# Twenty bf16 identity matmuls on TensorE at the start of each attention call

## The chip, the core and the metric

The kernel runs on one core of one Trainium2 chip. The metric is the device time of one execution in microseconds (us). Three runs of the kernel before took 1405.46, 1410.10 and 1411.19 us; their median is 1410.1 us. All computation is in one launch.

## The reference, cut to what matters

The reference is a decoder of four layers on x of 8 x 128 x 128 (batch B = 8, sequence S = 128, width D = 128). Each layer has an attention-like block, a cross block with a context of the same size, and a feed-forward block:

```python
x = x + L0_attn(layernorm(x), ...)        # mamba scan
x = x + L0_xattn(layernorm(x), ctx, ...)  # attention, rotary, masks     -> call 0
x = x + L0_ffn(layernorm(x), ...)         # experts
x = x + L1_attn(layernorm(x), ...)        # causal, relative positions   -> call 1
x = x + L1_xattn(...); x = x + L1_ffn(...)
x = x + L2_attn(layernorm(x), ...)        # causal, rotary               -> call 2
x = x + L2_xattn(...)
x = x + L2_ffn(layernorm(x), ...)         # holds a causal attention     -> call 3
x = x + L3_attn(layernorm(x), ...)        # two causal attentions        -> calls 4 and 5
x = x + L3_xattn(...); x = x + L3_ffn(...)
```

The change touches the softmax attentions, with 16 heads of 8 elements each:

```python
att = einsum("bhtd,bhsd->bhts", q, k) / sqrt(8) + bias   # 8 x 16 matrices of 128 x 128
out = einsum("bhts,bhsd->bhtd", softmax(masked(att)), v)
```

## The kernel before

The program is a row of stages, each a block in which the five engines run their own instruction queues and meet through semaphores; at a block's end all engines meet. The six attentions all go through one function, `attend` (L508), once per call. In front of it `attention_inputs` (L413) projects queries, keys and values; behind it `out_project` (L667) projects the result.

`attend` works through 32 units: a unit is one batch element and one group of four heads (HG = 4), that is four score matrices of 128 x 128, one bank of 128 x 512 f32 in PSUM. Four banks hold scores, two hold turned probabilities (`PT`), one holds the weighted sums (`PO`) and one, `back`, holds these sums turned back to token rows. All eight banks are in use. A unit passes through these steps:

- `add_bias` (TensorE, L546): mask or position bias, as bf16 matmuls of 512 columns into `scores`; one per unit with 64 rows in call 0, three per unit in call 1, one per unit (`identb` by a mask) in calls 2 to 5;
- `score` (TensorE, L553): queries against keys, f32, 32 rows of the array, into the same bank. The keys `KH` come from GpSimd (L537), spread by a head mask;
- `highest` (VectorE, L614): reduction for the softmax's shift; `exp` (ScalarE, L648): four activations;
- `turn` (TensorE, L561): four f32 transposes into `PT`; `copy` (VectorE, L620): to SBUF;
- `weigh` (TensorE, L570): 4 matmuls with the values into `PO`.

Once per batch element ScalarE evacuates `PO` (L656), TensorE turns it back into `back` (`turn_back`, L579), and VectorE divides by the sums of exponentials (L625, L626), reading `back`.

The order on TensorE is written out by hand. Biases and scores of units 0 to 3 come first. Then each pass of a loop takes two units: turn u and u+1, biases of u+4 and u+5, in some passes `turn_back`, scores of u+4 and u+5, and weighing of u-2 and u-1. So the passes u = 0 and u = 2 are the ones without a weighing or with the first one. TensorE's instructions start strictly in this order; a wait at the head holds all that is behind it. `back` is first written in the pass u = 6 (`turn_back(0)`, as `u % NG == 2 and u >= NG`).

`m.identb` (L163, filled at L283) is the 128 x 128 identity in bf16; `bcast_mid(x, n)` (L234) repeats x n times along the free dimension.

Of the kernel before, what the change touches and what calls it, by code (L numbers as in the profile page):

```python
# [27 lines left out]
HG = 4  # L28
# [205 lines left out]
def bcast_mid(ap, n):  # L234

    return ap.unsqueeze(1).to_broadcast([ap.shape[0], n, ap.shape[1]])


def bcast_last(ap, n):

    return ap.unsqueeze(2).to_broadcast([ap.shape[0], ap.shape[1], n])


def start_stage(nc, m):
# [263 lines left out]
def attend(nc, m, QT, KT, O, bias, beside=None):  # L508

    call = m.n_attn
    m.n_attn += 1
    U0, B0 = call * B * NG, call * B
    UNITS = B * NG
    with ExitStack() as ctx:
        sb = lambda name, shape, dt=F32: ctx.enter_context(nc.sbuf_tensor(f"{name}_a{call}", shape, dt))
        ps = lambda name, shape: ctx.enter_context(nc.psum_tensor(f"{name}{call}", shape, F32))
        KH = [sb(f"KH{i}", [D, HG, S]) for i in range(2)]
        shifted = [sb(f"shifted{i}", [S, HG, S]) for i in range(4)]  # L520
        PTs = [sb(f"PTs{i}", [S, HG, S]) for i in range(4)]
        POs = [sb(f"POs{i}", [128, NG, S]) for i in range(2)]
        nmax, rsum = sb("nmax", [S, 4, HG]), sb("rsum", [S, 2, H])
        scores = [ps(f"scores{i}_", [S, HG, S]) for i in range(4)]
        PT = [ps(f"PT{i}_", [S, HG, S]) for i in range(2)]
        PO, back = ps("PO", [128, NG, S]), ps("back", [S, NG, 128])
        block = ctx.enter_context(nc.Block())
        ident = m.w("ident")

        @block.gpsimd  # L530
        def _(pool):
            for b in range(B):
                if beside is not None and b >= 2:
                    beside(pool, b - 2)
                if b >= 2:
                    pool.wait_ge(m.scored, U0 + (b - 1) * NG)
                nc.gpsimd.tensor_tensor(KH[b % 2][:], bcast_mid(KT[:, b * S:(b + 1) * S], HG),  # L537
                                        bcast_last(m.w("head_mask"), S), ALU.mult).then_inc(m.kh_ready, 1)

        @block.tensor  # L540
        def _(pe):
            def add_bias(u):
                if u >= 4:
                    pe.wait_ge(m.exped, U0 + u - 3)
                for k, (w, x) in enumerate(bias(u % NG, u // NG)):
                    nc.tensor.matmul(scores[u % 4][:], w, x, start=(k == 0), stop=False)  # L546

            def score(u):
                g, b = u % NG, u // NG
                rows = slice(32 * g, 32 * g + 32)  # L550
                if g == 0:
                    pe.wait_ge(m.kh_ready, B0 + b + 1)
                nc.tensor.matmul(scores[u % 4][:], QT[rows, b * S:(b + 1) * S], KH[b % 2][rows, :, :], start=False,  # L553
                                 stop=True).then_inc(m.scored, 1)

            def turn(u):
                pe.wait_ge(m.exped, U0 + u + 1)
                if u >= 2:
                    pe.wait_ge(m.pt_copied, U0 + u - 1)
                for j in range(HG):  # L560
                    t = nc.tensor.transpose(PT[u % 2][:, j, :], shifted[u % 4][:, j, :], ident)  # L561
                t.then_inc(m.p_turned, 1)

            def weigh(u):
                g, b = u % NG, u // NG
                pe.wait_ge(m.pt_copied, U0 + u + 1)
                if g == 0 and b >= 1:
                    pe.wait_ge(m.po_copied, B0 + b)
                for j in range(HG):
                    t = nc.tensor.matmul(PO[32 * j:32 * j + 32, g, :], m.V[:, b, g * HG + j, :], PTs[u % 4][:, j, :],  # L570
                                         start=True, stop=True)
                t.then_inc(m.weighed, 1)

            def turn_back(b):
                pe.wait_ge(m.po_copied, B0 + b + 1)
                if b >= 1:
                    pe.wait_ge(m.out_done, B0 + b)
                for g in range(NG):
                    t = nc.tensor.transpose(back[:, g, :], POs[b % 2][:, g, :], ident)  # L579
                t.then_inc(m.turned_back, 1)  # L580

            for u in (0, 1):
                add_bias(u)
            for u in (0, 1):
                score(u)
            for u in (2, 3):
                add_bias(u)
            for u in (2, 3):
                score(u)
            for u in range(0, UNITS, 2):  # L590
                turn(u)
                turn(u + 1)
                if u + 4 < UNITS:
                    add_bias(u + 4)
                    add_bias(u + 5)
                if u % NG == 2 and u >= NG:
                    turn_back(u // NG - 1)
                if u + 4 < UNITS:
                    score(u + 4)
                    score(u + 5)  # L600
                if u >= 2:
                    weigh(u - 2)
                    weigh(u - 1)
            weigh(UNITS - 2)
            weigh(UNITS - 1)
            turn_back(B - 1)

        @block.vector
        def _(dve):
            def highest(u):  # L610
                if u >= 4:
                    dve.wait_ge(m.exped, U0 + u - 3)
                dve.wait_ge(m.scored, U0 + u + 1)
                nc.vector.tensor_reduce(nmax[:, u % 4, :], scores[u % 4][:], AX.X, ALU.min).then_inc(m.maxed, 1)  # L614

            def copy(u):
                dve.wait_ge(m.p_turned, U0 + u + 1)
                if u >= 4:
                    dve.wait_ge(m.weighed, U0 + u - 3)
                nc.vector.tensor_copy(PTs[u % 4][:], PT[u % 2][:]).then_inc(m.pt_copied, 1)  # L620

            def normalise(b):
                dve.wait_ge(m.turned_back, B0 + b + 1)
                po = back[:].rearrange("p g (j e) -> p (g j) e", j=HG)
                m.dve_steps.done(dve, nc.vector.reciprocal(rsum[:, b % 2, :], po[:, :, DH]))  # L625
                nc.vector.tensor_tensor(O[:, b, :].rearrange("p (h d) -> p h d", h=H), po[:, :, 0:DH],  # L626
                                        bcast_last(rsum[:, b % 2, :], DH), ALU.mult).then_inc(m.out_done, 1)

            for u in range(4):
                highest(u)  # L630
            for u in range(0, UNITS, 2):
                copy(u)
                copy(u + 1)
                for k in (u + 4, u + 5):
                    if k < UNITS:
                        highest(k)
                if u % NG == 2 and u > NG:
                    normalise(u // NG - 1)
            normalise(B - 1)

        @block.scalar
        def _(act):
            def exp(u):
                if u >= 4:
                    act.wait_ge(m.p_turned, U0 + u - 3)
                act.wait_ge(m.maxed, U0 + u + 1)
                for j in range(HG):
                    t = nc.scalar.activation(shifted[u % 4][:, j, :], scores[u % 4][:, j, :], ACT.Exp, scale=-1.0,  # L648
                                             bias=nmax[:, u % 4, j:j + 1])
                t.then_inc(m.exped, 1)  # L650

            def evacuate(b):
                act.wait_ge(m.weighed, U0 + (b + 1) * NG)
                if b >= 2:
                    act.wait_ge(m.turned_back, B0 + b - 1)
                nc.scalar.activation(POs[b % 2][:], PO[:], ACT.Copy).then_inc(m.po_copied, 1)  # L656

            m.load_table(act, ACT.Exp)
            for u in range(0, UNITS, 2):
                exp(u)  # L660
                exp(u + 1)
                if u % NG == 2 and u >= NG:
                    evacuate(u // NG - 1)
            evacuate(B - 1)
# [1666 lines left out]
```

## Time and profile before

| | |
|---|---|
| median of three runs | 1410.1 us |
| the profiled execution's own time | 1418.91 us |
| its span, first to last instruction | 1417.0 us |
| TensorE matmul, weight load | 1106.5 us (78%), 802.9 us (57%) |
| VectorE, ScalarE, GpSimd | 850.1 us (60%), 528.3 us (37%), 569.3 us (40%) |
| mean granted clock of TensorE | 0.825 |

| call of `attend` | 0 | 1 | 2 | 3 | 4 | 5 |
|---|---|---|---|---|---|---|
| its first matmul, us of the span | 452.20 | 589.40 | 804.34 | 930.56 | 1108.59 | 1168.91 |

The span is the time from the first to the last instruction of the one execution that the profiler recorded. Busy time is summed over an engine's instructions; a matmul's own duration holds its way through the array, so neighbours overlap, and the spacing of starts says more of the price than the duration. The granted clock is the share of 2.4 GHz that TensorE was given: 1.00 is 2.4 GHz, 0.50 is 1.2 GHz, and a value between the two in a slice is a mean over a change within it.

### The profile page before, as it was taken

The numbers are of one execution on the slowest core, as the hardware profiler recorded it, in microseconds if no ns is written. First come the engines' busy times: TensorE is split into PE (matmuls) and PEld (weight loads), VectorE is DVE, ScalarE is ACT, GpSimd is POOL, SyncE is SP. The second block draws the span as 40 slices with busy tenths as digits, with TensorE's granted clock in tenths as the row PEclk, the third lists the DMA queues.
The fourth block names the chain that finished last, engine by engine and source line by source line (L and its number), as shares of the span: only waits on it lengthen the run. The fifth ranks groups of instructions, "written<-read, shape, count | busy, mean of one in ns | idle before, by whom it ended". The sixth has DMA issues, their size and how long they took to land. (4 is left out here: it accounts for less than half of the span.)

```text
span 1417.0 us, 29481 instructions
## 1 busy us (share of the span) xinstructions
PE 1106.5 (78%) x11885; PEld 802.9 (57%) x11885; DVE 850.1 (60%) x1500; ACT 528.3 (37%) x1322; POOL 569.3 (40%) x382
## 2 busy tenths in 40 slices
PE   4479889998977989897465697599386889856795
PEld 1168878887874454555355255545275455533595
DVE  7577888888865674466522485557423576755233
ACT  2443444444331543363122172156143665512121
POOL 5079899899836403110345210110534101001332
PEclk9756888878886798999578698699588998977998
DMA  2098778777845000000274000000464000001683
GB/s 103 15 227 216 201 204 213 206 205 207 211 174 173 1 1 0 1 1 1 63 208 122 16 1 1 1 1 2 144 209 137 1 2 1 1 1 52 221 293 105
DMA packets 74230, 139.73 MB, mean 99 GB/s; under 512 B 8128, under 2 KB 28368, under 8 KB 73744
## 3 DMA queue, kind: packets, MB, share of 16 engines
q1 hardware_dynamic: 70128, 129.67, 32.2%
q0 software_dynamic: 3968, 8.18, 1.6%
q8 instruction: 95, 1.56, 0.5%
q14 instruction: 39, 0.32, 0.1%
HBM read 128.06 MB, written 14.82 MB: 101 GB/s over the span
## 5 line engine op out<-in xcount | busy, mean ns | idle before, releaser
L648 ACT ACTIVATE shifted_a<-scores,nmax_a 128x128 f32<-128x128 f32 x768 | 208.5, 387 | 85.5 <-DVE nmax_a L614 85.5
L1115 PE MATMUL decay<-delta,A_pairs 32*128 32x127 f32 x2048 | 176.1, 333 | 49.0 <-DVE small_pack L1209 19.8
L1190 ACT ACTIVATE decay<-decay 128x1016 f32<-128x1016 f32 x128 | 128.7, 1010 | 196.4 <-PE decay L1115 196.4
L1115 PEld LDWEIGHTS decay<-delta,A_pairs 32*128 32x128 f32 x2048 | 153.7, 233 | 69.2 <-DVE small_pack L1209 24.7
L614 DVE TENSOR_REDUCE nmax_a<-scores 128x4 f32<-128x512 f32 x192 | 123.6, 686 | 108.9 <-PE scores L553 106.5
L355 POOL TENSOR_TENSOR rstd<-ve,neghalf 128x4 f32<-128x4 f32 x30 | 31.5, 1050 | 284.5 <-DVE ve L341 284.5
L620 DVE COPY PTs_a<-PT 128x512 f32<-128x512 f32 x192 | 123.5, 680 | 3.4 <-PE PT L561 3.3
L1450 POOL DMA_INDIRECT results<-xs_s x76 | 72.8, 958 | 120.8 <-DVE xs_s L1622 114.4
L561 PE MATMUL PT<-mamba_pack,shifted_a 128*128 128x128 f32 x768 | 112.4, 290 | 4.3 <-DVE PTs_a L620 2.7
L561 PEld LDWEIGHTS PT<-mamba_pack,shifted_a 128*128 128x128 f32 x768 | 87.0, 147 | 36.7 <-issue 20.0
L1101 POOL TENSOR_TENSOR pos_bias<-pos_bias,B 128x1024 f32<-128x1024 f32 x36 | 85.0, 2381 | 11.0 <-DMA pos_bias<-du_rows 11.0
L361 PE MATMUL norm_ps<-mamba_pack,XN 128*128 128x128 f32 x96 | 29.2, 429 | 68.3 <-DVE XN L345 67.9
L553 PE MATMUL scores<-KH_a,QT_a 32*128 32x512 f32 x256 | 77.7, 685 | 1.0 <-POOL KH_a L537 1.0
L537 POOL TENSOR_TENSOR KH_a<-KT_a,small_pack 128x512 f32<-128x512 f32 x24 | 24.9, 1041 | 124.2 <-PE scores L553 99.8
L570 PEld LDWEIGHTS PO<-PTs_a,V 128*32 128x32 f32 x1536 | 36.9, 110 | 62.8 <-issue 33.4
L1132 PE MATMUL Y<-h,Cz 128*32 128x64 f32 x2048 | 63.7, 289 | 2.9 <-issue 2.4
L1132 PE MATMUL Y<-small_pack,Cz 128*32 128x64 f32 x2048 | 63.4, 289 | 1.2 <-issue 1.2
L1101 POOL TENSOR_TENSOR XN<-XN,B 128x1024 f32<-128x1024 f32 x19 | 45.2, 2379 | 45.2 <-DMA XN<-du_rows 45.1
L361 PEld LDWEIGHTS norm_ps<-mamba_pack,XN 128*128 128x128 f32 x96 | 16.2, 169 | 80.2 <-DVE XN L345 73.7
L570 PE MATMUL PO<-PTs_a,V 128*32 128x128 f32 x1536 | 61.5, 281 | 0.0
L1132 PEld LDWEIGHTS Y<-h,Cz 128*32 128x32 f32 x2048 | 55.4, 134 | 7.9 <-issue 4.5
L1132 PEld LDWEIGHTS Y<-small_pack,Cz 128*32 128x32 f32 x2048 | 54.9, 136 | 6.4 <-issue 4.0
(393 smaller groups left out, 2202.6 us busy)
## 6 DMA issues: line engine op xcount, KB each, us to landing
pos_bias<-du_rows SPq DMA_DIRECT2D x72, 256.0 KB, 4.8
small_pack<-L3f_w SPq DMA_DIRECT2D x15, 768.0 KB
XN<-du_rows SPq DMA_DIRECT2D x38, 256.0 KB, 4.9
XNT<-du_rows SPq DMA_DIRECT2D x38, 256.0 KB, 4.8
O<-du_rows SPq DMA_DIRECT2D x36, 256.0 KB, 4.7
masked_cos<-du_rows SPq DMA_DIRECT2D x36, 256.0 KB, 4.8
masked_sin<-du_rows SPq DMA_DIRECT2D x36, 256.0 KB, 4.7
small_pack<-L2f_w SPq DMA_DIRECT2D x15, 514.0 KB
```

What stands on the lines that cost most here:

```text
L361: t = nc.tensor.transpose(ps[:, b * S:(b + 1) * S], dst[:, b, :], m.w("ident"))
L553: nc.tensor.matmul(scores[u % 4][:], QT[rows, b * S:(b + 1) * S], KH[b % 2][rows, :, :], start=False, stop=True).then_inc(m.scored, 1)
L561: t = nc.tensor.transpose(PT[u % 2][:, j, :], shifted[u % 4][:, j, :], ident)
L570: t = nc.tensor.matmul(PO[32 * j:32 * j + 32, g, :], m.V[:, b, g * HG + j, :], PTs[u % 4][:, j, :], start=True, stop=True)
L614: nc.vector.tensor_reduce(nmax[:, u % 4, :], scores[u % 4][:], AX.X, ALU.min).then_inc(m.maxed, 1)
L620: nc.vector.tensor_copy(PTs[u % 4][:], PT[u % 2][:]).then_inc(m.pt_copied, 1)
L648: t = nc.scalar.activation(shifted[u % 4][:, j, :], scores[u % 4][:, j, :], ACT.Exp, scale=-1.0, bias=nmax[:, u % 4, j:j + 1])
L1101: nc.gpsimd.tensor_tensor(x, x, bcast_mid(B2[:, b * S:(b + 1) * S], PER), ALU.mult).then_inc(fed, 1)
L1115: t = nc.tensor.matmul(decay[k % DEEP][:, s, i, 1:S], A_pairs[strip, c, 4 * q + i, :, :].rearrange("p j n -> p (j n)"), delta[strip, c, b ...
L1132: t = nc.tensor.matmul(Y[32 * i:32 * i + 32, n % 2, half, :], Cz[:, token, :], at_token[n % 2][:, :, token], start=(turn == 0), stop=(turn ...
L1190: nc.scalar.activation(x, x, ACT.Exp).then_inc(decayed, 1)
L1450: nc.gpsimd.indirect_dma_start(results, bass.IndirectOffsetOnAxis(ap=number, axis=0), xs[:, j, 0:D], None).then_inc(returned.sem, returned ...
```

## The change

A helper issues a given number of matmuls of `identb` by four copies of `identb`, 128 x 512, bf16, each with `start` and `stop`, into a given tile. `attend` calls it three times on TensorE's queue, always into `back`: 8 times behind the scores of units 2 and 3 and ahead of the first turn, and 6 times behind the turns of each of the first two passes (u = 0 and u = 2), ahead of the biases of units 4, 5 and 6, 7. What they write is overwritten by `turn_back` before it is read. No semaphore, wait or transfer is added.

```diff
+def keep_awake(nc, m, out, times):
+
+    for _ in range(times):
+        nc.tensor.matmul(out, m.identb[:], bcast_mid(m.identb[:], HG), start=True, stop=True)
+
...
             for u in (2, 3):
                 score(u)
+            keep_awake(nc, m, back[:].rearrange("p g x -> p (g x)"), 8)
             for u in range(0, UNITS, 2):
                 turn(u)
                 turn(u + 1)
+                if u < 4:
+                    keep_awake(nc, m, back[:].rearrange("p g x -> p (g x)"), 6)
                 if u + 4 < UNITS:
                     add_bias(u + 4)
                     add_bias(u + 5)
```

## Rows read from the trace of the kernel before

Windows and slices: from:to, length, then busy time and count of PE, PEld, DVE, ACT and POOL, the granted clock, the DMA share and GB/s. Timelines: start, time, engine, line, operation, tiles, shapes, count, idle time before and its releaser.

**Rows 1.** Busy time and granted clock of two stretches (length, then busy and count).

```profile
453.00:476.40 23.40, 23.12 (x91) 10.44 (x92) 10.72 (x17) 10.10 (x37) 19.55 (x9) 0.50 0.01 3
935.00:958.40 23.40, 23.02 (x211) 13.27 (x210) 19.29 (x35) 17.84 (x64) 3.65 (x4) 1.00 0.01 2
```

**Rows 2.** The same view in slices of 3 us, where the clock rises.

```profile
474.00:477.00 3.00, 3.00 (x26) 2.13 (x24) 2.22 (x4) 1.99 (x7) 1.25 (x1) 0.59 0.00 0
...
814.00:817.00 3.00, 3.00 (x18) 1.32 (x14) 2.02 (x4) 1.22 (x5) 0.00 (x0) 0.93 0.00 0
...
925.00:928.00 3.00, 3.00 (x8) 1.32 (x8) 0.00 (x0) 1.54 (x3) 0.00 (x0) 0.66 0.00 0
...
1104.00:1107.00 3.00, 3.00 (x8) 1.29 (x6) 0.00 (x0) 1.96 (x4) 0.00 (x0) 0.91 0.00 0
...
1181.00:1184.00 3.00, 3.00 (x18) 1.29 (x20) 1.46 (x4) 1.87 (x8) 0.02 (x1) 0.66 0.01 3
```

**Rows 3.** Timeline, call 3, one round: weigh, turn, bias, score (start us, us, ...).

```profile
940.41 0.64 PE L570 MATMUL PO<-PTs_a,V 128*32 128x128 f32 x16
...
940.98 1.09 PE L561 MATMUL PT<-mamba_pack,shifted_a 128*128 128x128 f32 x8
...
941.91 0.59 PE L546 MATMUL scores<-causalb,identb 128*128 128x512 bf16 x2
...
942.44 1.13 PE L553 MATMUL scores<-KH_a,QT_b 32*128 32x512 f32 x4
...
943.49 0.64 PE L570 MATMUL PO<-PTs_a,V 128*32 128x128 f32 x16
```

**Rows 4.** Timeline, call 1: six bias matmuls, then the scores.

```profile
602.78 1.46 PE L546 MATMUL scores<-pos_part,flipb 128*128 128x512 bf16 x6
...
604.17 1.13 PE L553 MATMUL scores<-KH_a,QT_a 32*128 32x512 f32 x4
```

**Rows 5.** Timeline, call 1: first turns, then the bias.

```profile
594.30 1.31 PE L561 MATMUL PT<-mamba_pack,shifted_a 128*128 128x128 f32 x8
...
595.45 1.46 PE L546 MATMUL scores<-pos_part,flipb 128*128 128x512 bf16 x6
```

**Rows 6.** Timeline, call 3: second scores, first turn, bias.

```profile
933.24 1.13 PE L553 MATMUL scores<-KH_a,QT_b 32*128 32x512 f32 x4
...
934.78 0.66 PE L561 MATMUL PT<-mamba_pack,shifted_a 128*128 128x128 f32 x4 [0.42 <-ACT shifted_a L648]
...
936.31 0.59 PE L546 MATMUL scores<-causalb,identb 128*128 128x512 bf16 x2
```

**Rows 7.** Timeline, call 0: first turns, a pair of biases, scores, the later bias.

```profile
458.25 1.97 PE L561 MATMUL PT<-mamba_pack,shifted_a 128*128 128x128 f32 x8
...
465.01 1.03 PE L546 MATMUL scores<-k_mask,q_mask 64*128 64x512 bf16 x2
...
465.98 2.08 PE L553 MATMUL scores<-KH_a,QT_x 32*128 32x512 f32 x4
...
476.66 0.60 PE L546 MATMUL scores<-k_mask,q_mask 64*128 64x512 bf16 x2
```

**Rows 8.** Timeline of TensorE alone: two projections.

```profile
921.16 6.59 PE L446 MATMUL in_ps<-XNT,small_pack 128*128 128x512 f32 x8 [1.11 <-PEq L288]
...
1099.84 7.72 PE L446 MATMUL in_ps<-XNT,small_pack 128*128 128x512 f32 x12 [1.87 <-PEq L1343]
```

**Rows 9.** Timeline, calls 2 and 5: first and third turns.

```profile
810.40 1.97 PE L561 MATMUL PT<-mamba_pack,shifted_a 128*128 128x128 f32 x8
...
817.90 1.09 PE L561 MATMUL PT<-mamba_pack,shifted_a 128*128 128x128 f32 x8
...
1174.97 1.97 PE L561 MATMUL PT<-mamba_pack,shifted_a 128*128 128x128 f32 x8
...
1184.37 1.09 PE L561 MATMUL PT<-mamba_pack,shifted_a 128*128 128x128 f32 x8
```

## The prediction, made blind

> **What bounds the kernel now.** The first view to open is the busy time and granted clock of stretches. In the middle of a call of `attend`, TensorE is busy 23.02 of 23.40 us at a granted clock of 1.00, with VectorE at 19.29, ScalarE at 17.84 and GpSimd at 3.65 [rows 1]. So TensorE's own queue sets the pace of a call, and what is added to that queue is paid unless TensorE stood waiting at that place. The same view over the start of the first call (call 0) shows the second thing to see: 23.12 of 23.40 us busy, but at a clock of 0.50 (1.2 GHz), with 91 matmuls done against 211 in as long a stretch at 1.00 (2.4 GHz) [rows 1]. Half-clock spells inside calls are all that this change could win back.
>
> The second view is the clock in slices of 3 us. A mean of 0.59 between two levels 0.50 and 1.00 puts the rise at (0.59 - 0.50) / 0.50 of the slice before its end. That gives 476.5 in call 0, 814.4 in call 2 and 1183.0 in call 5 [rows 2]. Calls 1, 3 and 4 have clock 1.00 throughout, because the clock had already risen in the projections before them (927.0 and 1104.5 for calls 3 and 4, [rows 2]). The page's strip of clock says the same in coarse slices. The third view is the timeline of TensorE around the first turns. Its rows give the prices and show where TensorE waits. The chain of waits is of little use here: it is broken at the stages' ends and names each line with 1% or less.
>
> **The change, part by part.** It removes and moves nothing, adds no wait or semaphore, and touches no DMA. It adds per call 8 + 6 + 6 = 20 matmuls of 128x512 bf16 (I call the three groups A, B, C), 120 over six calls. They write `back`, which nobody reads before the first `turn_back`; that one comes behind them in the same queue, so no wait is born there.
>
> *Price of one.* The shape runs already, as the bias of the scores (L546). Two of them take 942.44 - 941.91 = 0.53 us from first start to the next block's start [rows 3]; six of them 604.17 - 602.78 = 1.39 [rows 4]. The four more cost 0.86, so 0.215 us each at full clock. At half clock a pair takes 465.98 - 465.01 = 0.97 [rows 7], 0.22 more for each, so 0.43 each. At full clock A is 1.72 us, B and C 1.29 each, 4.30 in all; at half clock A is 3.44. The spacings hold the weight loads too.
>
> *Price of the other blocks at full clock* [rows 3]: weigh 0.57, turn (a pair of units, 8 transposes) 0.93, bias 0.53, score 943.49 - 942.44 = 1.05.
>
> *Calls 1, 3 and 4 (full clock).* Here the only cover is time in which TensorE waits. In call 1 the first turns take from 594.30 to the bias at 595.45, 1.15 against the dense 0.93: 0.22 is wait on the exponentials, which A hides [rows 5]. Net 4.30 - 0.22 = +4.1. In call 3, scores issued at 933.24 would be done issuing at 934.29; the bias starts at 936.31, 2.02 later against 0.93, so 1.09 of wait goes under A [rows 6]. Net +3.2. Call 4 repeats the pattern of call 3, +3.2. Nothing hides B and C: the exponentials of the second pair of units are ready by then. Behind that, the calls are TensorE-bound and nothing gives the time back. Sum of the three: **+10.5**.
>
> *Calls 0, 2 and 5 (half clock).* Let r be how long the clock stays low once A begins. Bounds for r: nothing at the least; at the most what a dense projection needed, 921.16 to 927.0, 5.9 us, and 1099.84 to 1104.5, 4.7 us [rows 2 and 8]. I take 3.0, the middle, as no row shows these matmuls waking the clock. A low clock doubles the time, so it costs r/2 = 1.5 over the full-clock sum.
> - Call 0, from A's place (458.25) to the bias behind the fourth turn (476.66): 18.41 before [rows 7]. After: A 1.72, four turns 3.72, B and C 2.58, three biases 1.59, three scores 3.15, two weighs 1.14 = 13.90, plus 1.5 = 15.40. **-3.0**.
> - Call 2, from 810.40 to the third turn at 817.90: 7.50 before [rows 9]. After: 1.72 + two turns 1.86 + 2.58 + two biases 1.06 + two scores 2.10 + weigh 0.57 = 9.89, plus 1.5 = 11.39. **+3.9**. This clock rose 4.0 us behind A's place by itself.
> - Call 5, the same blocks, from 1174.97 to 1184.37: 9.40 before [rows 9], 11.39 after. **+2.0**.
>
> Total 10.5 - 3.0 + 3.9 + 2.0 = **+13.4 us**. With r = 0 it is 8.9; with r = 5.9, 17.8. Against the profiled execution (span 1417.0, its own time 1418.9) that is 1432.3. The runs' median is 1410.1, 8.8 lower; I carry the difference over, so 1423.5.
>
> The sections before each A stay at half clock either way: A begins 6 us after a call's first matmul.
>
> **A rule weighed.** In call 0 TensorE is full for 23 us at 0.50, with four turns of eight f32 transposes in the 18.4 us behind 458.25 [rows 1, 7]. The Trainium skill (TensorE: Matmul & The Clock Gate, "Part 4: PE-mode transpose") says that the full clock does not engage for transpose mode, since it isn't counted as busy. That speaks for the change; by it alone every call would be low. Call 3, with the same transposes, holds 1.00 [rows 1], so the trace bears it out in part only. The same page ("Back-to-back issue gap") gives ~131 ns for each of a sustained stream of matmuls of 512 columns; an estimate from it is 120 x 0.084 = 10.1 us less, +3.3 in all. This trace shows 0.215.
>
> **Rivals.**
> 1. *The added matmuls cost less than the bias ones*, as all have one weight. The nearest lower row is a transpose in a dense turn, 0.93 / 8 = 0.116. 120 x 0.099 = 11.9 less: +1.5, time 1411.6, within the noise. Against it: the pairs and sixes of bias also repeat the same weight. Chance 0.05.
> 2. *They do not wake the clock.* Then all 20 cost 0.43 in the three low calls, 8.6 each: 10.5 + 25.8 = +36.3, time 1446. Against it: the clock rises in calls 2 and 5 with far fewer such matmuls. Chance 0.04.
> 3. *Faster: ordinary executions sit low in every call as call 0 does here*, because the gap at a call's start drops the clock and score and transposes don't raise it. Then each call gains 3.0: -18, time 1392. It decides from four calls out of six (4 x 3.0 against 2 x 3.5). For it: three of six calls are low here and the place of a rise differs (18, 4 and 8 us behind A's place). Against it: calls 1, 3 and 4 start only about 1 us behind a projection that had woken the clock. Chance 0.05. If calls 1, 3 and 4 are only as low as call 5, each costs 2.0 and the total is +8.9.
> 4. *Re-timing*: later stages start at other moments, and a low spell of call 0's size (18.4 us at half clock, 9 more than at full) comes or goes there. +4 or +22, time 1414 or 1432. Chance 0.08.
>
> **How the numbers follow.** My forecast holds 0.78. Time **1423.5**. The range takes in r's bounds (1419 to 1428), the case of calls as low as call 5, and re-timing at both ends: 1414 to 1432. What a measurement of this kernel can tell from no change is about 0.5%, 7 us, so 1403 to 1417. Faster 0.06 (rival 3 and a little of 4); same 0.10 (rival 1, half of 4, and a tail of the forecast); slower 0.84.
>
> **What would show it.** 120 new bf16 matmuls in `back`, 0.215 us apart at clock 1.00. In calls 1, 3 and 4, counted from the call's first matmul, the first turn starts 1.7 us later or (calls 3 and 4) 1.2, and the third turn 4.1, 3.2 and 3.2 later. In call 0 the clock rises less than 6 us behind the first of them, and the bias behind the fourth turn starts some 21.5 us after the call's first matmul instead of 24.5. Rounds in the middle of calls stay at 3.08 us. I am wrong if rounds shrink or a stage without new matmuls moves by more than some us, if calls 1, 3 or 4 are the same length (hidden cover I missed), or if calls 2 and 5 get shorter.

## The result and the profile after

| | before | after |
|---|---|---|
| median, 8 runs each | 1408.94 us | 1418.53 us |
| lowest and highest | 1405.14, 1411.19 | 1414.15, 1427.10 |
| span of the profiled execution | 1417.0 us | 1416.3 us |
| mean granted clock | 0.825 | 0.835 |

The ratio is 1.0088, 95% interval 1.0069 to 1.0107: slower by 12.4 us (9.7 to 15.1). The two medians alone are 9.6 us apart, just under the low edge of that interval. A second comparison (below) gave 1.0098 (1.0065 to 1.0132). Forecast: slower, 1423.5 us, +13.4; the median came out 5 us under the forecast time.

The two spans are no sign that nothing happened. Cut the timelines into calls (from the first bias matmul to the end of the last division into O) and the stages between them:

| us | call 0 | 1 | 2 | 3 | 4 | 5 | all calls | gap ahead of call 2 | tail behind call 5 |
|---|---|---|---|---|---|---|---|---|---|
| before | 68.8 | 69.3 | 60.0 | 56.9 | 56.9 | 61.9 | 373.7 | 145.7 | 186.1 |
| before, second trace | 68.8 | 69.0 | 62.0 | 56.9 | 56.9 | 61.8 | 375.4 | 137.9 | 178.4 |
| after | 66.9 | 73.1 | 64.7 | 60.0 | 60.0 | 64.5 | 389.3 | 137.0 | 179.1 |
| after, second trace | 66.7 | 73.1 | 63.3 | 60.0 | 60.0 | 64.6 | 387.7 | 146.5 | 186.7 |
| forecast for after | 65.8 | 73.4 | 63.9 | 60.1 | 60.1 | 63.9 | 387.1 | | |

The calls are 15.6 us longer than in the first trace of before and 13.9 longer than in the second. One caution on call 1: its first bias block has six matmuls, and every trace but the first of before holds a record of only five. So its 69.3 is counted from one matmul, 0.22 us, earlier than its 69.0 and 73.1. Like for like, call 1 is 4.05 us longer, and the calls 15.8 and 13.9.

The first trace of before had two expert stages together 15.6 us longer than after (8.6 and 7.0, in the last two columns); a second trace of the same kernel has them short, and one of after has them long. Between two traces of one kernel each scatters by 7.6 to 9.5 us, so they say nothing of the change.

Where the time goes in a call at full clock is plain in the timeline of TensorE in call 3 (start us, us, engine, line, operation, tiles, shapes, count). The helper's line is L247; add_bias is now L552, score L559, turn L567, weigh L576:

```profile
930.14 1.13 PE L559 MATMUL scores<-KH_a,QT_b 32*128 32x512 f32 x4
931.20 1.90 PE L247 MATMUL back<-identb 128*128 128x512 bf16 x8
932.94 1.04 PE L567 MATMUL PT<-mamba_pack,shifted_a 128*128 128x128 f32 x8
933.81 1.46 PE L247 MATMUL back<-identb 128*128 128x512 bf16 x6
935.11 0.59 PE L552 MATMUL scores<-causalb,identb 128*128 128x512 bf16 x2
935.63 1.13 PE L559 MATMUL scores<-KH_a,QT_b 32*128 32x512 f32 x4
936.69 1.09 PE L567 MATMUL PT<-mamba_pack,shifted_a 128*128 128x128 f32 x8
937.62 1.46 PE L247 MATMUL back<-identb 128*128 128x512 bf16 x6
938.91 0.59 PE L552 MATMUL scores<-causalb,identb 128*128 128x512 bf16 x2
939.44 1.13 PE L559 MATMUL scores<-KH_a,QT_b 32*128 32x512 f32 x4
940.49 0.65 PE L576 MATMUL PO<-PTs_a,V 128*32 128x128 f32 x16
941.07 1.09 PE L567 MATMUL PT<-mamba_pack,shifted_a 128*128 128x128 f32 x8
942.00 0.59 PE L552 MATMUL scores<-causalb,identb 128*128 128x512 bf16 x2
942.52 1.13 PE L559 MATMUL scores<-KH_a,QT_b 32*128 32x512 f32 x4
943.58 0.65 PE L576 MATMUL PO<-PTs_a,V 128*32 128x128 f32 x16
```

Eight added matmuls take 932.94 - 931.20 = 1.74 us and six 935.11 - 933.81 = 1.30: the price by [rows 3, 4]. No idle time stands at any of these rows; the wait for the exponentials of [rows 6] is gone, filled. The next round, 943.58 - 940.49 = 3.09 us, is what it was in [rows 3] (3.08). So the delay is kept to the call's end.

In a call that starts low, here call 0:

```profile
452.30 0.73 PE L552 MATMUL scores<-k_mask,q_mask 64*128 64x512 bf16 x2 [3.00 <-PEq L430]
...
458.36 3.59 PE L247 MATMUL back<-identb 128*128 128x512 bf16 x8
461.74 1.59 PE L567 MATMUL PT<-mamba_pack,shifted_a 128*128 128x128 f32 x8
463.17 1.46 PE L247 MATMUL back<-identb 128*128 128x512 bf16 x6
```

The first eight take 461.74 - 458.36 = 3.38 us (forecast 3.44 at half clock), and the clock rises inside the turns behind them. The view of busy time and clock by slices says when, for calls 0, 2 and 5 (length, busy time and count of PE, PEld, DVE, ACT, POOL, then the clock):

```profile
461.00:464.00 3.00, 3.00 (x15) 2.08 (x14) 1.16 (x2) 0.35 (x2) 2.92 (x2) 0.69 0.00 0
...
806.00:809.00 3.00, 3.00 (x16) 2.17 (x15) 1.34 (x2) 0.00 (x0) 0.00 (x0) 0.73 0.00 0
...
1182.00:1185.00 3.00, 3.00 (x17) 2.04 (x15) 1.29 (x2) 0.00 (x0) 0.00 (x0) 0.82 0.00 0
```

Worked as in the prediction, the rises are at 462.9, 807.6 and 1183.1, and the first added matmuls stand at 458.36, 802.85 and 1178.69: r is 4.5, 4.8 and 4.4 us. Against [rows 2], call 0's rise came 4.5 us behind A's place instead of 18.2.

### The profile page after: what moved, and what is told of

It is laid out like the page before. It is cut to its first block and busy times, and to the rows that moved or that the text cites. A ratio compares the mean times of both kernels' runs of the same rounds, so it can differ in the third digit from the quotient of the medians.

```text
span 1416.3 us, 29710 instructions
## 1 busy us (share of the span) xinstructions
PE 1115.0 (79%) x11994; PEld 805.4 (57%) x12005; DVE 849.0 (60%) x1500; ACT 528.7 (37%) x1322; POOL 569.3 (40%) x382
## 5 line engine op out<-in xcount | busy, mean ns | idle before, releaser
L1124 PEld LDWEIGHTS decay<-delta,A_pairs 32*128 32x128 f32 x2048 | 154.0, 233 | 69.6 <-DVE small_pack L1218 23.9
L629 DVE COPY PTs_a<-PT 128x512 f32<-128x512 f32 x192 | 122.8, 680 | 13.5 <-PE PT L567 13.5
L567 PE MATMUL PT<-mamba_pack,shifted_a 128*128 128x128 f32 x768 | 107.1, 282 | 2.7 <-DVE PTs_a L629 2.7
L567 PEld LDWEIGHTS PT<-mamba_pack,shifted_a 128*128 128x128 f32 x768 | 84.6, 143 | 27.2 <-issue 21.4
L559 PE MATMUL scores<-KH_a,QT_a 32*128 32x512 f32 x256 | 75.9, 671 | 1.0 <-POOL KH_a L543 1.0
L576 PEld LDWEIGHTS PO<-PTs_a,V 128*32 128x32 f32 x1536 | 36.5, 109 | 61.2 <-issue 33.6
L576 PE MATMUL PO<-PTs_a,V 128*32 128x128 f32 x1536 | 60.6, 278 | 0.0
```

The lines of the kernel that those rows point to most:

```text
L1124: t = nc.tensor.matmul(decay[k % DEEP][:, s, i, 1:S], A_pairs[strip, c, 4 * q + i, :, :].rearrange("p j n -> p (j n)"), delta[strip, c, b ...
```

## The experiments

"Kernel before" runs beside each set on the same chip; its medians differ from set to set (1404 to 1425 us, and 1404 and 1424 in two sets on one chip), so ratios are given. The table holds the traces' call lengths; texts and verdicts follow.

| kernel | ratio (95% interval) | call 0 | 1 | 2 | 3 | 4 | 5 | sum |
|---|---|---|---|---|---|---|---|---|
| the kernel before again | 1.001 (0.999, 1.003) | 68.8 | 69.0 | 62.0 | 56.9 | 56.9 | 61.8 | 375.4 |
| change in calls 0, 2, 5 | 1.0041 (1.0019, 1.0062) | 66.9 | 69.0 | 64.7 | 56.9 | 56.9 | 64.6 | 379.0 |
| change in calls 1, 3, 4 | 1.0096 (1.0066, 1.0126) | 68.8 | 73.1 | 62.0 | 60.0 | 60.0 | 61.7 | 385.7 |
| the same, doubled | 1.0198 (1.0164, 1.0232) | 68.8 | 77.4 | 61.9 | 64.4 | 67.7 | 59.9 | 400.0 |
| the change again | 1.0098 (1.0065, 1.0132) | 66.7 | 73.1 | 63.3 | 60.0 | 60.0 | 64.6 | 387.7 |
| A only | 1.0014 (0.9993, 1.0035) | 64.1 | 70.5 | 60.7 | 60.7 | 60.7 | 61.6 | 378.3 |
| B and C only | 1.0041 (1.0017, 1.0066) | 65.2 | 71.6 | 61.6 | 59.4 | 59.4 | 61.6 | 378.9 |
| A in call 0 only | 0.9948 (0.9919, 0.9976) | 64.3 | 69.0 | 59.0 | 56.9 | 56.9 | 61.9 | 368.0 |
| in the gaps ahead of 0, 2, 5 | 0.9911 (0.9877, 0.9945) | 64.9 | 69.0 | 56.9 | 56.9 | 56.9 | 56.9 | 361.4 |
| gaps, and 2 in each call's first wait | 0.987 (0.9839, 0.9901) | 59.2 | 69.5 | 56.9 | 56.9 | 56.9 | 56.9 | 356.1 |
| gaps and waits | 0.9869 (0.9833, 0.9904) | 59.2 | 69.0 | 56.9 | 56.9 | 56.9 | 56.9 | 355.7 |
| gaps, waits, normalisations | 0.9804 (0.9777, 0.9832) | 59.2 | 69.0 | 56.9 | 56.9 | 56.9 | 56.9 | 355.7 |

**The kernel before, unchanged.** No edit.

> The kernel before, once more, for a second trace. Two stages without any new matmul (the experts of layer 1, and those of layer 3) were 8.6 and 7.0 us longer in the trace of before than in that of after. Theory A (scatter between executions, by the transfers of the experts' weights): this trace has at least one of the two shorter, and the ratio is 1.000. Rival B (the change itself made these stages shorter, by moving when their work meets the clock or the transfers): this trace repeats both long values, the gap between calls 1 and 2 near 145.7 us and the tail behind call 5 near 186 us. Calls 0 to 5 are 68.8, 69.3, 60.0, 56.9, 56.9 and 61.9 us long, within 2 us for 0, 2 and 5 and 0.3 for the others.

137.9 and 178.4 us: both long stages are gone, so theory A. The same trace shows how call 2 varies by itself: its clock stayed low for 13.7 us instead of 10.2 and rose 14.4 us behind its first matmul instead of 10.1, and it took 62.0 us instead of 60.0. So the first trace flattered call 2 of the kernel before by 2 us. Three more kernels below leave call 2 as it was: it took 62.0, 61.9 and 59.0 us.

**The change by kind of call.** In `attend`, the two calls of the helper get a condition, here for the first of the kernels:

```diff
+            if call in (0, 2, 5):
                 keep_awake(nc, m, back[:].rearrange("p g x -> p (g x)"), 8)
...
-                if u < 4:
+                if u < 4 and call in (0, 2, 5):
```

> Matmul groups A, B, C only in calls 0, 2 and 5, which start at half clock. Theory (a call's cost is its own and adds up): calls change by -1.9, +4.7, +2.6 as in the trace of the whole change, +5.4 us, ratio 1.004; calls 1, 3 and 4 stay at 69.3, 56.9 and 56.9. Rival (the whole change was paid in the calls at full clock alone, and at half clock it breaks even or wins): ratio 1.000 or below.

> The groups only in calls 1, 3 and 4, which start at full clock. Theory: they can't gain there and cost +3.8, +3.2 and +3.2, 10.2 us, ratio 1.007. Rival (the delay is partly given back behind the calls, as transfers for the next stage have longer): the calls are that much longer but the time rises by under 6 us. Second rival (in ordinary executions these calls fall to half clock now and then, and the groups prevent it): under 7 us as well, but with the calls of the trace shorter than 73.1, 60.0 and 60.0.

> As before but with 16, 12 and 12 matmuls in calls 1, 3 and 4. Theory (0.215 us for each, no cover left once the first group has filled the wait): each call is 4.3 us longer than with 8, 6 and 6, so +23.1 us against the kernel before, ratio 1.016. Rival (a run of matmuls with one weight gets cheaper as it gets longer): under 3 us more a call, ratio under 1.013.

The low calls alone cost 5.8 us by the ratio (2.7 to 8.7). Their own lengths rise by 5.5 against the first trace of before and by 3.6 against the second, and the interval holds both. The calls at full clock alone cost 13.5 us by the ratio (9 to 18); their own lengths rise by 4.05, 3.2 and 3.2 (call 1 like for like), 10.4 in all. That refutes giving back, and it speaks against the groups protecting these calls from something, as they are exactly as long as the sum says. Doubling adds 4.3 us in calls 1 and 3, so a longer run gets no cheaper. The ratio, 1.0198, is above the forecast 1.016. Call 4 is 7.6 longer, and this was in no theory: its clock fell 2.5 us into the call, ahead of the first added matmul. The slices of call 4 in the doubled kernel:

```profile
1116.00:1119.00 3.00, 2.72 (x8) 0.92 (x10) 1.29 (x2) 1.42 (x6) 1.22 (x2) 0.78 0.00 0
1119.00:1122.00 3.00, 3.00 (x9) 0.72 (x6) 1.29 (x2) 2.58 (x11) 1.04 (x1) 0.50 0.02 5
```

The call began at 1115.20 and group A at 1120.00. So a call like 3 or 4 can fall in its own first passes (pairs of biases, scores on 32 rows, waits), and group A comes too late to prevent it.

**The change once more**, without an edit.

> The change itself once more, beside the others on one chip and for a second trace. Theory (costs of calls add up): calls 66.9, 73.1, 64.7, 60.0, 60.0 and 64.5 us, stages between them as in the second trace of the kernel before (gap to call 2 near 137, tail near 176), so ratio 1.009 to 1.011. Rival (the two half changes, 1.004 and 1.010, stand for more than the whole because something is given back): 1.006 or less.

Ratio 1.0098, calls as in the first trace but for call 2 at 63.3, whose clock was low for 6.8 us only. The halves' ratios add to 1.0137, and their two intervals together are wide enough for 1.0098. The calls' lengths add up as well: against the second trace of before the halves are 3.6 and 10.3 us longer, together 13.9, and the whole change 13.9 in its first trace and 12.3 in this one. So nothing shows a giving back.

**One group at a time.** Remove the other helper call.

> Only group A, 8 matmuls ahead of the first turn. Theory (A alone wakes the clock about 4.2 us behind its start, B and C are pure cost): calls 1, 3 and 4 change by +1.5, +0.6, +0.6; calls 0, 2 and 5 are 2.6 us shorter than with the whole change, so 64.3, 62.1 and 61.9. Sum of the calls -1.9 us against the second trace of before, ratio 0.999. Rival (A is not enough: without B the clock stays low past the first turns): calls 0, 2 and 5 have the clock at 0.50 beyond 5 us behind A's start and are 1 to 3 us longer than that.

> Only groups B and C, 6 matmuls behind the turns of each of the first two passes. Theory: calls 1, 3 and 4 change by +2.6 each, as the exponentials are ready by then and the wait ahead of the first turns stays where it was; in call 0 the clock rises behind B, some 6 us behind the place of A, and the call is about 66 us; call 2 is about 64, call 5 about 63. Sum near +8 us, ratio 1.006. Rival (B and C cost less than A because the transposes' waits cover them): calls 1, 3 and 4 by under +1.5.

A alone is enough: call 0 takes 64.1 us, and its clock was low for 10.2 us as with all three groups. Call 1 is 1.5 longer, as forecast. The forecast of calls 3 and 4 (+0.6) failed: +3.8 and +3.9. Their clock fell 1.8 and 2.2 us into the call:

```profile
930.00:933.00 3.00, 2.51 (x8) 0.44 (x7) 0.62 (x2) 0.10 (x1) 1.94 (x2) 0.79 0.02 5
933.00:936.00 3.00, 3.00 (x7) 0.78 (x7) 1.31 (x4) 2.18 (x8) 0.55 (x1) 0.50 0.00 0
936.00:939.00 3.00, 3.00 (x11) 1.36 (x10) 0.65 (x2) 2.18 (x8) 0.49 (x1) 0.57 0.00 0
```

This is call 3 of the kernel with A alone, from 929.91; A stands at 935.26, behind the fall. It is the same event as in call 4 of the doubled kernel. In these three calls the clock had risen 4.3 to 5.0 us ahead of the call's first matmul; in the calls 3 and 4 that held without anything added in their first wait, 3.5 to 4.2 us ahead.

B and C alone cost 2.59 and 2.58 in calls 3 and 4, which is 12 x 0.215 = 2.58 and settles that nothing covers them. With them call 0 is short as well, 65.2 us: 3.6 less than before, and 1.7 less than with the whole change, as A's work is saved. Here the clock rose at 464.8, only 2.7 us behind B's first matmul at 462.16, and 10.5 us behind the call's first matmul, about where it rose with A:

```profile
464.00:467.00 3.00, 3.00 (x14) 0.98 (x13) 0.38 (x1) 0.00 (x0) 3.00 (x1) 0.86 0.00 0
```

So the moment of the rise doesn't simply follow the first added matmul. Calls 2 and 5 are 61.6 us each, less than the forecast 64 and 63: their clock rose 0.5 and 0.8 us behind B.

**A in call 0 only.** As above, with `if call == 0:` ahead of A, no B and C.

> Group A alone and in call 0 alone, the one place where the whole change gained. Theory: call 0 takes 64.1 to 64.4 us instead of 68.8, nothing else moves, ratio 0.9965. Rival (a gain in a call is lost behind it, as a transfer or the next stage's clock sets the end): call 0 as short as that, but the gap behind it or a later stage longer by as much, ratio 1.000.

Call 0 is 4.5 us shorter and the others as before but for call 2, 59.0. Nothing is added in call 2 here, and yet its clock rose at 811.1, 8.2 us behind its first matmul at 802.92:

```profile
810.00:813.00 3.00, 3.00 (x16) 1.49 (x15) 1.84 (x4) 1.72 (x7) 0.00 (x0) 0.81 0.00 0
```

The ratio 0.9948 (0.9919 to 0.9976) is more than 4.5 us would give (0.9968), but its interval holds that. The gain is not lost behind the call. With A in all its calls and B and C, the change has much the same gain in call 0 and pays some four times as much elsewhere (13.9 + 4.5 = 18.4 us).

**Matmuls where TensorE idles.** Instead of groups in the calls, the helper runs at the end of `attention_inputs` for calls 0 and 2 and behind the transposes ahead of call 5, each into a bank that nobody uses:

```diff
             for u in range(slots, len(units)):
                 product(u)
+            if turn:
+                keep_awake(nc, m, idle[:], 12)
...
                         t = nc.tensor.transpose(later[0:S - 1, b, :], m.XNT[:, b * S + 1:(b + 1) * S], m.w("ident"))
                     t.then_inc(m.proj, 1)
+                    keep_awake(nc, m, idle[:], 8)
```

> No group A, B or C. Instead 12 such matmuls behind the last projection of the two calls with rotary inputs (0 and 2), where TensorE idles 3 us while VectorE and GpSimd finish, and 8 behind the transposes ahead of call 5, where it idles 2 us; all into an unused bank. Theory (the clock falls because TensorE idles there, and a call at full clock from its first matmul takes 56.9 us): they cost nothing, calls 0, 2 and 5 come to 57 us, -21 us against the second trace of before, ratio 0.985. Rival (the low activity at the start of a call drops the clock anyway, whatever runs ahead): calls 0, 2 and 5 as before, ratio 1.000; a stage made longer by the matmuls would show as a larger gap ahead of those calls.

Calls 2 and 5 are 56.9 us, as forecast to 0.1. The timeline of TensorE ahead of call 5, first in the kernel before, then here:

```profile
1165.77 1.12 PE L1978 MATMUL later<-mamba_pack,XNT 128*127 128x128 f32 x8 [0.94 <-PEq L516]
1168.91 0.59 PE L546 MATMUL scores<-strictb,identb 128*128 128x512 bf16 x2 [2.01 <-PEq L1973]
```

```profile
1164.21 1.12 PE L1988 MATMUL later<-mamba_pack,XNT 128*127 128x128 f32 x8 [0.94 <-PEq L525]
1165.17 1.89 PE L247 MATMUL idle_later<-identb 128*128 128x512 bf16 x8
1167.36 0.59 PE L555 MATMUL scores<-strictb,identb 128*128 128x512 bf16 x2 [0.30 <-PEq L1983]
1168.44 1.13 PE L562 MATMUL scores<-KH_a,QT_a 32*128 32x512 f32 x4 [0.48 <-POOL KH_a L546]
```

From the transposes to the call's first matmul it is 3.15 us, against 3.14 in the trace of before (1165.77 to 1168.91): the eight matmuls are free, and the wait of 2 us is down to 0.30. The twelve are free too: ahead of calls 0 and 2, the last projections start 6.61 and 6.60 us before the call's first matmul, against 6.60 in both in the trace of before. Call 0 is where the forecast failed, 64.9 instead of 57, and the rival was right for this call: it started at full clock at 457.14, and the clock fell 4.0 us later. So the ratio is 0.9911, where 0.985 was forecast.

**Two more in the wait for the first keys; and four in the wait for the first exponentials.** The two stand behind the first two biases, the four behind the scores of units 2 and 3. The first kernel has the two in every call, the second has both groups in every call but call 1; this is the second's edit.

```diff
             for u in (0, 1):
                 add_bias(u)
+            if call != 1:
+                keep_awake(nc, m, back[:].rearrange("p g x -> p (g x)"), 2)
...
             for u in (2, 3):
                 score(u)
+            if call != 1:
+                keep_awake(nc, m, back[:].rearrange("p g x -> p (g x)"), 4)
```

> As the kernel with the matmuls in the stages' gaps, and 2 more in every call behind the first two biases, where TensorE waits about 0.5 us for the first spread keys. There call 0 had begun at full clock and fallen about 4 us into the call (64.9 us). Theory (it falls because its first passes are light: half-height biases and waits): 2 more matmuls may or may not carry it; if they do, call 0 is 57 us, and the others stay at 56.9, but call 1, which has no such wait, is 0.4 longer. Rival (call 0 falls whatever is put at its start, its own passes being too light): 64 to 65 us again.

> The gaps, 2 matmuls in the wait for the keys and 4 in the wait for the first exponentials, in all calls but call 1. Both waits were measured: 0.5 us and 1.09 us, against 0.43 and 0.86 us of matmuls. Theory (matmuls are free in a wait and hold the clock): calls 0, 2, 3, 4 and 5 all 56.9 to 57.1 us, call 1 69.0; 11 us less than the second trace of before in call 0 alone, ratio 0.982 to 0.985. Rival (call 0's clock falls later still, once the waits are over): call 0 at 62 us or more with the clock low from its second pass.

Two matmuls in the first wait (0.43 us of work in a wait of 0.5) carry call 0 through: 59.2 us in both kernels, no low clock. The fall without them stands in one trace. The ratios bear it out, though their intervals overlap: 0.9911 and 0.987 are 5.8 us apart, and call 0 is 5.7 us shorter. Calls 3 and 4 of the first kernel held as well, though their clock had risen 4.7 and 4.4 us ahead of them, as early as in the calls that fell above; so this is the place where added matmuls may protect such a call. Call 0 is 9.6 us shorter than before and stays 2.3 above the 56.9 of the other calls, for its rounds are longer at the same clock. In the timeline of the kernel with gaps and waits:

```profile
466.65 0.65 PE L579 MATMUL PO<-PTs_a,V 128*32 128x128 f32 x16
467.22 1.09 PE L570 MATMUL PT<-mamba_pack,shifted_a 128*128 128x128 f32 x8
468.25 0.60 PE L555 MATMUL scores<-k_mask,q_mask 64*128 64x512 bf16 x2
468.78 1.13 PE L562 MATMUL scores<-KH_a,QT_x 32*128 32x512 f32 x4
469.84 0.65 PE L579 MATMUL PO<-PTs_a,V 128*32 128x128 f32 x16
```

The round is 3.19 us against 3.09, and all of the difference is in the turn, 1.03 against 0.93. Sixteen turns make 1.6 of the 2.3; what makes them longer here isn't shown. The four more matmuls change nothing that these traces show. In call 1 of the first kernel, without that wait, the two cost 0.4 us (69.5 against 69.0), as forecast. The slices of call 0 in the kernel with gaps and waits, to hold against the first of [rows 1], where as long a stretch did 91 matmuls:

```profile
456.60:480.00 23.40, 23.35 (x172) 11.23 (x174) 16.84 (x28) 16.07 (x59) 23.00 (x11) 1.00 0.03 8
```

**The same idea in the normalisations.** 12 matmuls ahead of the transposes of each normalisation fused behind another stage:

```diff
         def _(pe):
+            if complete is not None:
+                keep_awake(nc, m, ps[:, 0:HALF], 12)
             for b in range(B):
                 pe.wait_ge(m.normed, n * B + b + 1)
```

> The kernel with matmuls in the gaps and waits of the calls, and 12 more in every normalisation that is fused behind another stage, ahead of its transposes, where TensorE waits for VectorE (3.8 us behind call 0, 2.6 us behind a sum of products); they write the bank that the transposes fill next. Theory (a wait that ends at half clock doubles what follows): behind call 0 the eight transposes (2.5 us at half clock) and the next stage's first 5 us of matmuls start at full clock; 2 to 4 us less for each of some six normalisations, ratio 0.97 to 0.98. Rival (VectorE and ScalarE bound these stages, or the clock has fallen already when the matmuls start, so that they take 5.2 us instead of 2.6 and delay the transposes): ratio 0.985 to 0.992, with transposes later than before in the stages whose clock is low.

The fastest kernel: 0.9804 of before, 1393.9 us where before is 1421.7 on that chip, mean clock 0.859. That lies below the rival's 0.985 and at the edge of the theory's 0.97 to 0.98. Behind call 0 the mechanism brought nothing: TensorE still waits 1.19 us between the added matmuls and the transposes, the transposes wait for VectorE one by one, and the clock falls at 516.2 (0.60 in the slice from 516 to 517), so that the next stage starts low and its first row takes as long as before (3.55 against 3.56 us). From the product ahead of the added matmuls (`tail_y`) to that row it is 518.32 - 509.07 = 9.25 us, against 526.68 - 517.44 = 9.24 in the kernel with gaps and waits. The timeline of TensorE there, then here:

```profile
517.44 2.05 PE L705 MATMUL tail_y<-small_pack,OT 128*128 128x128 f32 x16 [0.25 <-ACT OT L713]
523.26 2.50 PE L367 MATMUL norm_ps<-mamba_pack,XN 128*128 128x128 f32 x8 [3.77 <-DVE XN L351]
526.68 3.56 PE L1318 MATMUL logits<-small_pack,XNT 128*128 128x8 f32 x16 [0.93 <-PEq L685]
```

```profile
509.07 2.05 PE L707 MATMUL tail_y<-small_pack,OT 128*128 128x128 f32 x16 [0.25 <-ACT OT L715]
510.96 2.75 PE L247 MATMUL norm_ps<-identb 128*128 128x512 bf16 x12
514.90 1.10 PE L369 MATMUL norm_ps<-mamba_pack,XN 128*128 128x128 f32 x4 [1.19 <-DVE XN L351]
516.15 1.24 PE L369 MATMUL norm_ps<-mamba_pack,XN 128*128 128x128 f32 x4
518.32 3.55 PE L1320 MATMUL logits<-small_pack,XNT 128*128 128x8 f32 x16 [0.93 <-PEq L687]
```

So the 9 us over the kernel before it came elsewhere. In the traces call 0 begins at 448.2 us (451.8 to 457.1 in the other thirteen), and from call 0 to call 1 it is 65.1 us (66.6 to 68.7 in the others). Which stages in these stretches gained was not taken apart, and the two kernels ran in different sets on different chips.

## Why the prediction was right

*TensorE's queue sets a call's pace.* Right, down to the signs named in advance: counted from the call's first matmul, the first turn is 1.7 us later in call 1 (1.7 expected; against the second trace of before, which lacks the same record) and 1.25 in call 3 (1.2). Calls 3 and 4 are 3.2 us longer in both traces of the change, forecast 3.2; call 1 4.05, forecast 4.1. Rounds stay at 3.09.

*Price 0.215 us, 0.43 at half clock.* Right: 1.30 for six, 3.38 for eight at half clock. Rival 1 (cheaper matmuls) is out by the doubled kernel and by B and C alone. The Trainium skill's ~131 ns for 512 columns in a sustained stream (TensorE: Matmul & The Clock Gate, "Back-to-back issue gap") is not seen here: 12 more cost 2.58 us.

*They wake the clock, r = 3.0.* In call 0, right in kind and small in size. Its clock rose 24.2 to 24.3 us behind its first matmul in the four traces without groups there, and after 10.0 to 10.6 us in the six with A or B in it. In calls 2 and 5 it is less plain: with groups the clock rose after 8.0 to 10.9 us (ten calls), without anything added before or in them after 8.2 to 14.4 us (ten calls, of which three after 8.2 to 10.1). So there the groups rather cut off the long spells, and one early rise proves nothing. The sizes of r are 4.5, 4.8 and 4.4 in the first trace of the change, and 4.0, 2.2 and 4.5 in the second. Each us of r was priced at one half, so the first trace's are +0.75, +0.9, +0.7 on the three low calls, 2.35 in all; 13.4 + 2.35 = 15.75 against the 15.8 of the first traces. Measured for call 0: -1.9 (forecast -3.0), call 2: +4.7 (+3.9), call 5: +2.6 (+2.0). Of the 1.1 us in call 0, 0.4 is no matter of r: the sum priced its four turns at 0.93 us, from call 3, and in call 0 a turn takes 1.03 at full clock.

*The spell of before as the other side of the sum.* Here the one trace was lucky: call 2 is 2 us longer in the second trace. With that the calls' difference is 13.9, and the time changed by 12.4 (9.7 to 15.1). So r too small and a short spell in call 2 erred in opposite senses, and the total is nearer to the forecast than its parts. That part of the agreement is luck.

*Rival 2* (no waking) is out by the rises in call 0 and by the time: its +36 us is far outside the interval. *Rival 3* (ordinary executions low in every call) is out: calls 1, 3 and 4 of both traces of before are at full clock. But its mechanism exists: in two of the fourteen traces calls 3 or 4 fell (three calls), each time ahead of group A, so that the change gives no protection against such a fall. *Rival 4* (later stages re-timed): scatter of 7.6 to 9.5 us in expert stages was there, in both kernels, and not from the change.

*The transpose rule.* The Trainium skill (TensorE: Matmul & The Clock Gate, "Part 4: PE-mode transpose") says that full clock does not engage for transposes. No call here bears that out: once up, calls 2 to 5 hold 1.00 to their end with eight transposes in each 3.09 us round. What keeps call 0 low for longer than call 2, no run isolates.

## What to carry to other kernels

A matmul that keeps TensorE's clock up is free only where TensorE already waits; put ahead of ready work it costs its full spacing, and half of the low spell that it must outlast on top. So look for the idle gap behind which the clock falls, fill that one with as many matmuls as fit, and leave calls that hold their clock alone: the same instruction gave +0.9% behind the first scores, -0.9% in the gaps ahead of the calls, and -1.3% with two more in each call's first wait. Before counting a saved spell as a gain, take a second trace of the kernel before; the spell of one call differed by 3.4 us between two executions of one program. And before taking a difference of 0.2 us from two traces, count the records of the first block: one can be missing.

## What the runs showed of the hardware

- TensorE can be busy and still be granted half clock. Call 0 of before stayed at 0.50 for 23.9 us, busy 99% of it [rows 1], with biases of 64 rows and f32 scores of 32 rows. Call 2 has biases of 128 rows, and its spells lasted 6.8 to 13.7 us where nothing was added. The two calls differ in more than that (GpSimd too is busy 19.55 of 23.40 us in call 0, against 3.65 in call 3 [rows 1]), so that the rows are the cause is not shown.
- With six or eight bf16 matmuls of 128 rows and 512 columns added at 6 to 8 us into call 0, its clock rose 10.0 to 10.6 us into it instead of 24.2 to 24.3, in six traces of six. From the first added matmul to the rise it was 4.0 to 4.6 us with A and 2.7 with B.
- A call at full clock can fall while TensorE is busy 2.51 of 3.00 us, with 32-row scores and short waits. Two bf16 matmuls (0.43 us) in the first wait went with a call 0 that stayed up, in three traces of three; without them it fell, in one of one.
- Spells in calls lasted 6.8, 10.2, 13.7 or 23.9 us, and one of 17.1 began 3.4 us ahead of its call. The same call of the same program showed two of these values.
- Added identity matmuls at full clock cost 0.215 us each, whether 2, 6, 8 or 16 stand in a row (1.30 for six, 1.74 for eight, 937.68 - 934.21 = 3.47 for sixteen in call 3 of the doubled kernel).
